# Delta-rule attention layer on one chip: gate stage and l2norms moved in the block head, two filters' spectral products separated

## The chip, the cores and the metric
One Trainium2 chip, 8 cores. Every core runs the same program on one of the 8 batch rows (2048 tokens of 1024 features); the cores exchange nothing. The metric is the device time in microseconds of the slowest core. The profile is of that core (core 5) in one execution.

## The reference
One layer with adaptive layer norm (shift, scale and gate from a conditioning row), an attention part and a feed-forward part. Shortened:

```
h = layernorm(x) * (1 + ca) + sa
q, k, v = [silu(causal_dwconv(h @ W, conv4))  for W in (Wq, Wk, Wv)]    # 4 heads x 256
beta = sigmoid(h @ Wb);  w_global = sigmoid(h @ Wg + bg);  p = softmax((h @ Wl + bl) / temp)
q, k = l2norm(q), l2norm(k)                        # per head
o_d  = delta rule over q, k, v, beta               # chunkwise, state S of 256 x 256 per head
local = p0 * v + p1 * fir_short(v) + p2 * fir_long(v)     # 3 and 31 taps, causal
o = rmsnorm(w_global * o_d + (1 - w_global) * local) @ Wo
x = x + ga * o
h = layernorm(x) * (1 + cb) + sb
x = x + gb * tanh(h @ W @ A1 @ A2 + bias)
```

## The kernel before
A core works through its 2048 tokens in 4 blocks of 512 (`for b in range(NB)`). A block has a head, four chunks of 128 tokens, and the feed-forward part.

**How the order is set.** Each stage is queued with `st(engine, counter, waits, instructions)`; every engine runs its stages in the order in which the program queues them, and a stage waits for the marks named in it. So an instruction that waits holds up everything queued behind it on its engine. A stage counts once, at its last instruction. Weight loads are issued from GpSimd's queue, each after the previous one has landed, two halves of `w_str` in turn.

**The head.** `ln_and_h` normalizes the block and leaves h in `h_blk`. `project` computes one of q, k, v: four groups of two column blocks (PSUM `ps_p`, `ps_q`), each group with two half loads of weights, 16 matmuls (L539), and two ScalarE copies into `z_blk` (L553), which also wait for the mark `z_free`. Then VectorE does the 4-tap convolution into `y_blk` (L565, L573), and ScalarE applies Silu (L585). `z_free` is set when the convolution has read `z_blk`. `l2norm` squares q or k (VectorE, L591), sums by matmul (L593), takes Ln and Exp on ScalarE (L600, L603), and for each of four heads copies the factor to all partitions by an fp32 matmul (L614), copies it to SBUF `rs_rep` (ScalarE, L620) and multiplies (VectorE, L624). `bgl_stage` computes the gates: 8 matmuls from `h_blk` (L637), a ScalarE copy of the logits into a part of `rs_rep` (L643), four transposes (L646), and a chain of small steps on VectorE and ScalarE (L652 to L692). The order is: project q, l2norm q, gates, project k, l2norm k, project v.

**A chunk.** K and v are transposed to token-major (L741, L757) and copied and scaled by beta (L748, L749, L764, L765). The two filters are applied as products in the frequency domain: forward transform (L775, L782), three copies (L790 to L792), then for the long (f = 0) and the short filter (f = 1) six VectorE products and sums each (L806 to L824), an inverse transform of the long one (L828), its ScalarE copy to `ls_tm` (L836), the same for the short one in the same PSUM (L838, L846), and the mix (L849, L855, L862). Then the output projection of the chunk before is queued (`emit_tail`: transposes, ScalarE copy L708, 16 matmuls L711, residual add L719). Then come the 128 x 128 triangular inverse by six squarings (L871 to L940), the delta rule with its state update (L950 to L1032), and the RMS norm of the result (L1043 to L1055). `z_blk` also serves as scratch (`wfm`, `attnT`) in the chunks.

Of the kernel before, what the change touches and what calls it, by code (L numbers as in the profile page):

```python
# [9 lines left out]
ALU = mybir.AluOpType  # L10
# [150 lines left out]
def build_nc():  # L161
# [40 lines left out]
    with _stack:  # L202
# [26 lines left out]
        kh_blk = _stack.enter_context(nc.sbuf_tensor("kh_blk", [128, 4096], BF16))  # L229
        v_blk = _stack.enter_context(nc.sbuf_tensor("v_blk", [128, 4096], BF16))  # L230
# [5 lines left out]
        zh_k = _stack.enter_context(nc.sbuf_tensor("zh_k", [128, 32], BF16))  # L236
        zh_v = _stack.enter_context(nc.sbuf_tensor("zh_v", [128, 32], BF16))
# [24 lines left out]
        xhat = _stack.enter_context(nc.sbuf_tensor("xhat", [128, 2048], BF16))  # L262
# [32 lines left out]
        PE = Ctr(_pe); DVE = Ctr(_dve); ACT = Ctr(_act)  # L295
        LD = Ctr(_ld, 16); GLD = Ctr(_gld, 16); ST = Ctr(_st, 16)
        LDX = Ctr(_ldx, 16); GLD1 = Ctr(_gld1, 16)
        st = sch.stage
# [44 lines left out]
        m_wh = wh_last  # L343
# [19 lines left out]
        for q in range(4):  # L363
# [44 lines left out]
        m_clamp = st("vector", DVE, [m_cl3], [  # L408
            lambda e: e.tensor_tensor(ga_row, absrow, sgnrow, ALU.mult)])
# [22 lines left out]
        m_gates = st("vector", DVE, [m_g3], [  # L432
            lambda e: e.tensor_tensor(gates_fm[:, 40:48], st6[:, 0:8], st6[:, 8:16], ALU.mult)])
# [22 lines left out]
        state = {  # L456
            "m_h": m_consts, "m_x": m_x,
            "wstr_free": m_consts,
            "psg_free": m_gates, "pstr_free": m_wofold,
            "pspq_free": [m_mod, m_mod],  # L460
            "psu_free": m_wh, "pso_free": m_gar, "ofm_free": m_hist0,
            "m_S": m_hist0, "m_vtmprev": m_hist0, "m_mix_done": m_hist0,
            "m_clamp": m_clamp,
            "ln_free": m_gates,
            "y_free": m_hist0,
            "z_free": m_hist0,
        }
# [121 lines left out]
        def l2norm(src, m_src):  # L589
            sq = st("vector", DVE, [m_src, state["y_free"]], [  # L590
                lambda e: e.tensor_tensor(y_blk[:], src[:], src[:], ALU.mult)])  # L591
            smm = st("tensor", PE, [sq, state["psg_free"]], [
                (lambda e, g=g: e.matmul(ps_g[0:4, 0:512], onesl2_sb[:, 4 * g:4 * g + 4],  # L593
                                         y_blk[:, 512 * g:512 * (g + 1)],
                                         start=(g == 0), stop=(g == 7)))
                for g in range(8)
            ])
            state["y_free"] = smm
            rt0 = st("scalar", ACT, [smm], [
                lambda e: e.activation(rs4[0:4, 0:512], ps_g[0:4, 0:512],  # L600
                                       AF.Ln, bias=epsc_sb[0:4, 1:2])])
            rt = st("scalar", ACT, [rt0], [
                lambda e: e.activation(rs4[0:4, 0:512], rs4[0:4, 0:512],  # L603
                                       AF.Exp, scale=epsc_sb[0:4, 4:5])])
            state["psg_free"] = rt
            rc = rt
            marks = []
            for h in range(4):
                half = h % 2
                waits = [rc, state["pso_free"]]  # L610
                if len(marks) >= 2:
                    waits.append(marks[-2])
                rep = st("tensor", PE, waits, [
                    (lambda e, h=h, half=half: e.matmul(  # L614
                        ps_o[:, 512 * half:512 * (half + 1)],
                        onehot4_sb[:, 128 * h:128 * (h + 1)], rs4[0:4, 0:512],
                        start=True, stop=True))
                ])
                evr = st("scalar", ACT, [rep], [
                    (lambda e, half=half: e.copy(rs_rep[:, 512 * half:512 * (half + 1)],  # L620
                                                 ps_o[:, 512 * half:512 * (half + 1)]))
                ])
                ap = st("vector", DVE, [evr], [
                    (lambda e, h=h, half=half: e.tensor_tensor(  # L624
                        src[:, 1024 * h:1024 * (h + 1)].rearrange("p (c t) -> p c t", c=2),
                        src[:, 1024 * h:1024 * (h + 1)].rearrange("p (c t) -> p c t", c=2),
                        rs_rep[:, 512 * half:512 * (half + 1)].unsqueeze(1)
                        .broadcast_to([128, 2, 512]),
                        ALU.mult))
                ])  # L630
                marks.append(ap)
            state["pso_free"] = marks[-1]
            return marks[-1]
# [93 lines left out]
        for b in range(NB):  # L727
            ln_and_h(b, 0)
            m_q = project(b, "wq", qh_blk, zh_q, 0)
            m_ql2 = l2norm(qh_blk, m_q)  # L730
            m_bgl = bgl_stage(m_ql2)
            m_k = project(b, "wk", kh_blk, zh_k, 32)
            m_kl2 = l2norm(kh_blk, m_k)
            m_v = project(b, "wv", v_blk, zh_v, 64)

            for n in range(NCB):
                cofs = 128 * n
# [49 lines left out]
                    for ns in range(2) for kc in range(2)  # L787
                ])
                exh = st("vector", DVE, [ffw], [
                    lambda e: e.tensor_copy(xhat[:, 0:1024], ps_u[:, 0:1024]),  # L790
                    lambda e: e.tensor_copy(xhat[:, 1024:1536], ps_g[:, 0:512]),
                    lambda e: e.tensor_copy(xhat[:, 1536:2048], ps_p[:, 0:512]),  # L792
                ])
# [7 lines left out]
                _yh = (yhat[:], yhat2)  # L801
                _whf = (whl_sb, whs_sb)
                _sc = (mscr[:, 0:1024], mscr[:, 1024:2048])
                cm1 = st("vector", DVE, [exh, m_wh, state["m_mix_done"], state["m_clamp"],
                                         state["psu_free"]],
                    [(lambda e, f=f: e.tensor_tensor(  # L806
                        _yh[f][:, 0:1024], xhat[:, 0:1024], _whf[f][:, 0:1024], ALU.mult))
                     for f in range(2)]
                  + [(lambda e, f=f: e.tensor_tensor(
                        _sc[f], xhat[:, 1024:2048], _whf[f][:, 1024:2048], ALU.mult))  # L810
                     for f in range(2)]
                  + [(lambda e, f=f: e.tensor_tensor(
                        _yh[f][:, 1024:2048], xhat[:, 0:1024], _whf[f][:, 1024:2048], ALU.mult))
                     for f in range(2)])
                cm2 = st("vector", DVE, [cm1],
                    [(lambda e, f=f: e.tensor_sub(
                        _yh[f][:, 0:1024], _yh[f][:, 0:1024], _sc[f]))
                     for f in range(2)])
                cm3 = st("vector", DVE, [cm2],
                    [(lambda e, f=f: e.tensor_tensor(  # L820
                        _sc[f], xhat[:, 1024:2048], _whf[f][:, 2048:3072], ALU.mult))
                     for f in range(2)])
                cm = st("vector", DVE, [cm3],
                    [(lambda e, f=f: e.tensor_add(  # L824
                        _yh[f][:, 1024:2048], _yh[f][:, 1024:2048], _sc[f]))
                     for f in range(2)])
                im = st("tensor", PE, [cm, state["psu_free"]], [
                    (lambda e, ns=ns, part=part: e.matmul(  # L828
                        ps_u[:, 512 * ns:512 * (ns + 1)],
                        (dftir_sb if part == 0 else dftii_sb)[:, :],  # L830
# [352 lines left out]
```

How the kernel before makes its waits and increments, by code:

```python
        def fn(e):  # L144
            for c, v in wlist:
                if v > 0:
                    e.wait_ge(c.h, v)
            last = None
            for g in emits:
                last = g(e)
                if per_instr:
                    last.then_inc(ctr.h, ctr.step)
            if not per_instr:
                last.then_inc(ctr.h, ctr.step)
# [985 lines left out]
        def fin(e):  # L1140
            e.wait_ge(ST.h, ST.n)
```

## Time and profile before

| what | value |
|---|---|
| median of 3 runs (lowest, highest) | 2979.19 us (2978.45, 2985.77) |
| the profiled execution | 2974.76 us, span on core 5 2973.2 us |
| spans of the 8 cores | 2966.5 to 2973.2 us |
| TensorE busy | 1234.3 us, 42% of the span |
| VectorE busy | 1040.0 us, 35% |
| ScalarE busy | 405.8 us, 14% |
| GpSimd busy | 120.6 us, 4% |
| granted TensorE clock, mean | 0.66 of full speed |

Engines are called PE (TensorE matmul), PEld (weight load), DVE (VectorE), ACT (ScalarE), POOL (GpSimd), SP in the rows. L539 is line 539 of the kernel. Times in the rows are microseconds from the span's start. The chain of waits is followed back from the last instruction, at each step to what released it.

### The profile page before, as it was taken

The numbers are of one execution on the slowest core, as the hardware profiler recorded it, in microseconds if no ns is written. First come the engines' busy times: TensorE is split into PE (matmuls) and PEld (weight loads), VectorE is DVE, ScalarE is ACT, GpSimd is POOL, SyncE is SP. The second block draws the span as 40 slices with busy tenths as digits, with TensorE's granted clock in tenths as the row PEclk, the third lists the DMA queues.
The fourth block names the chain that finished last, engine by engine and source line by source line (L and its number), as shares of the span: only waits on it lengthen the run. The fifth ranks groups of instructions, "written<-read, shape, count | busy, mean of one in ns | idle before, by whom it ended". The sixth has DMA issues, their size and how long they took to land.

```text
span 2973.2 us, 16737 instructions; the slowest of 8 cores (2966.5 to 2973.2 us)
## 1 busy us (share of the span) xinstructions
PE 1234.3 (42%) x5208; PEld 549.7 (18%) x5208; DVE 1040.0 (35%) x1904; ACT 405.8 (14%) x547; POOL 120.6 (4%) x232
## 2 busy tenths in 40 slices
PE   1223442444454442444354433344454344344444
PEld 0001111222212111222211111222211111222211
DVE  1002336555301334555301333555501233555501
ACT  0002211000112211000112121000022221000021
POOL 0010000000010000000010000000000000000000
PEclk9999665555576666565576666565577676555567
DMA  7442120000032111000033222000023222000023
GB/s 177 74 75 29 23 29 12 0 1 0 5 56 60 25 28 25 0 1 0 1 50 64 29 28 29 0 1 0 0 43 71 28 29 29 0 1 1 0 35 71
DMA packets 38650, 83.95 MB, mean 28 GB/s; under 512 B 5084, under 2 KB 5503, under 8 KB 38438
## 3 DMA queue, kind: packets, MB, share of 16 engines
q0 software_dynamic: 32624, 65.14, 15.2%
q1 hardware_dynamic: 5942, 17.74, 1.7%
q8 instruction: 47, 0.77, 0.1%
q14 instruction: 37, 0.30, 0.0%
HBM read 139.60 MB, written 8.39 MB: 50 GB/s over the span
## 4 chain that ended last, share of the span: by engine, by line
DVE 29%; PE 26%; DMA 26%; issue 9%; ACT 8%; DVEq 0%; ACTq 0%; POOLq 0%; POOL 0%
DMA w_str<-wf_a 8%; DVE y_blk L573 7%; DMA z_blk<-wmod 5%; DMA w_str<-wk 3%; DMA w_str<-wq 3%; DMA w_str<-wv 3%; DMA w_str<-wf_w 3%; PE ps_o L711 3%; DVE Pp L923 2%; PE ps_o L614 2%; PE ps_g L932 2%; DVE Qp L926 2%; ACT h_blk L508 2%; DVE st L474 1%; ACT y_blk L492 1%
## 5 line engine op out<-in xcount | busy, mean ns | idle before, releaser
L573 DVE SCALAR_TENSOR_TENSOR y_blk<-z_blk,convw_sb,y_blk 128x512 bf16<-128x512 bf16 x288 | 194.0, 746 | 4.5 <-DVE y_blk L573 0.5
L539 PE MATMUL ps_p<-h_blk,w_str 128*128 128x512 bf16 x384 | 127.6, 465 | 151.9 <-DMA w_str<-wk 49.3
L1111 DVE TENSOR_SCALAR y_blk<-y_blk,gates_fm 128x512 bf16<-128x512 bf16 x32 | 11.3, 353 | 493.7 <-ACT y_blk L1107 493.7
L539 PE MATMUL ps_q<-h_blk,w_str 128*128 128x512 bf16 x384 | 133.8, 485 | 0.0
L593 PE MATMUL ps_g<-y_blk,onesl_sb 128*4 128x512 bf16 x64 | 28.3, 621 | 225.0 <-DVE y_blk L591 225.0
L932 PE MATMUL ps_g<-Rt,Pp 128*128 128x128 bf16 x384 | 56.2, 300 | 141.6 <-DVE Qp L926 123.7
L502 PE MATMUL ps_tr<-eye_sb,y_blk 128*128 128x128 bf16 x256 | 32.4, 307 | 155.3 <-ACT y_blk L492 114.8
L940 DVE TENSOR_TENSOR Rt<-Rt,ps_g 128x512 bf16<-128x512 bf16 x96 | 66.0, 687 | 80.9 <-PE ps_g L932 80.9
L711 PE MATMUL ps_o<-wo_sb,ofm_sb 128*128 128x512 bf16 x256 | 84.9, 505 | 22.4 <-ACT ofm_sb L708 22.4
L757 PE MATMUL ps_tr<-eye_sb,v_blk 128*128 128x128 bf16 x128 | 16.2, 306 | 184.3 <-ACT v_blk L585 100.4
L828 PE MATMUL ps_u<-yhat,dftir_sb 128*128 128x512 bf16 x32 | 19.5, 609 | 176.1 <-DVE mix_b L824 176.1
L539 PEld LDWEIGHTS ps_p<-h_blk,w_str 128*128 128x128 bf16 x384 | 36.1, 108 | 241.0 <-issue 225.6
L978 ACT CAST dtiles<-ps_u 128x512 bf16<-128x512 f32 x16 | 9.4, 585 | 513.2 <-PE ps_u L970 513.2
L1079 POOL DMA_DIRECT2D w_str<-wf_w x32 | 16.9, 528 | 1519.5 <-PE ps_q L1088 1407.5
L923 DVE CAST Pp<-ps_p 128x512 bf16<-128x512 f32 x96 | 66.3, 690 | 27.0 <-PE ps_q L915 27.0
L553 ACT CAST z_blk<-ps_p 128x512 bf16<-128x512 f32 x48 | 28.1, 585 | 325.2 <-PE ps_q L539 325.2
L1088 PE MATMUL ps_p<-kh_blk,w_str 128*128 128x512 bf16 x128 | 43.5, 474 | 67.4 <-DMA w_str<-wf_a 52.4
L379 PE MATMUL ps_g<-z_blk,cfm_sb 128*1 128x512 bf16 x32 | 18.7, 584 | 125.6 <-DMA z_blk<-wmod 125.6
L562 DVE TENSOR_TENSOR z_blk<-zh_q 128x32 bf16<-128x32 bf16 x4 | 0.7, 176 | 200.5 <-ACT z_blk L553 200.5
L1088 PE MATMUL ps_p<-qh_blk,w_str 128*128 128x512 bf16 x128 | 44.5, 483 | 62.4 <-DMA w_str<-wf_a 58.3
L614 PE MATMUL ps_o<-rs,onehot_sb 4*128 4x512 f32 x64 | 58.1, 1069 | 24.9 <-ACT rs L603 24.9
L1088 PE MATMUL ps_p<-h_blk,w_str 128*128 128x512 bf16 x128 | 46.7, 503 | 52.2 <-DMA w_str<-wf_w 43.3
(224 smaller groups left out, 2447.5 us busy)
## 6 DMA issues: line engine op xcount, KB each, us to landing
w_str<-wf_a POOLq DMA_DIRECT2D x64, 256.0 KB, 3.8
z_blk<-wmod POOLq DMA_DIRECT2D x32, 384.0 KB, 4.4
x_tm<-x SPq DMA_DIRECT2D x1, 8192.0 KB, 31.1
w_str<-wq POOLq DMA_DIRECT2D x32, 256.0 KB, 3.8
w_str<-wk POOLq DMA_DIRECT2D x32, 256.0 KB, 3.8
w_str<-wv POOLq DMA_DIRECT2D x32, 256.0 KB, 3.8
w_str<-wf_w POOLq DMA_DIRECT2D x32, 256.0 KB, 3.8
out<-x_tm SPq DMA_DIRECT2D x4, 2048.0 KB, 6.6
```

The costliest lines, as they stand in the source:

```text
L474: (lambda e, n=n, hf=hf: e.bn_stats(st6[:, 12 * n + 6 * hf: 12 * n + 6 * hf + 6], x_tm[:, xofs + 1024 * n + 512 * hf: xofs + 1024 * n + 51 ...
L502: (lambda e, g=g, n=n: e.transpose(ps_tr[:, 512 * (g % 2) + 128 * n: 512 * (g % 2) + 128 * (n + 1)], y_blk[:, 1024 * n + 128 * g: 1024 * n ...
L508: (lambda e, g=g: e.activation(h_blk[:, 512 * g:512 * (g + 1)], ps_tr[:, 512 * (g % 2):512 * (g % 2) + 512], AF.Identity, bias=gates_fm[:, ...
L539: (lambda e, g=g, mh=mh, hb=hb, pp=pp: e.matmul(pp[:, 0:512], halves[hb][:, 256 * (g - 4 * hb) + 128 * mh: 256 * (g - 4 * hb) + 128 * mh + ...
L573: (lambda e, g=g, j=j: e.scalar_tensor_tensor(y_blk[:, 512 * g:512 * (g + 1)], z_blk[:, 516 * g + j + 1: 516 * g + j + 513], convw_sb[:, c ...
L614: (lambda e, h=h, half=half: e.matmul(ps_o[:, 512 * half:512 * (half + 1)], onehot4_sb[:, 128 * h:128 * (h + 1)], rs4[0:4, 0:512], start=T ...
L711: (lambda e, g=g, sl=sl: e.matmul(ps_o[:, 512 * sl:512 * (sl + 1)], ofm_sb[:, 128 * g:128 * (g + 1)], wo_sb[:, 1024 * g + 512 * sl: 1024 * ...
L923: (lambda e, pn=pnx: e.tensor_copy(Pp[:, 512 * pn:512 * (pn + 1)], ps_p[:, 0:512])),
L926: (lambda e, qn=qnx: e.tensor_copy(Qp[:, 512 * qn:512 * (qn + 1)], ps_q[:, 0:512])),
L932: (lambda e, h=h, pn=pnx, rc=rcur: e.matmul(ps_g[:, 128 * h:128 * (h + 1)], Pp[:, 512 * pn + 128 * h: 512 * pn + 128 * (h + 1)], Rt[:, 512 ...
L940: (lambda e, rc=rcur, rn=rnx: e.tensor_add(Rt[:, 512 * rn:512 * (rn + 1)], Rt[:, 512 * rc:512 * (rc + 1)], ps_g[:, 0:512]))
L1088: (lambda e, g=g, mh=mh, hb=hb, pp=pp, src=src: e.matmul(pp[:, 0:512], halves[hb][:, 256 * (g - 4 * hb) + 128 * mh: 256 * (g - 4 * hb) + 1 ...
```

## The change
Two parts. In the head, the gate stage is queued right behind the q projection, the k and v projections follow, and both l2norms stand behind them, q's first. The gate stage's copy of the logits, which writes `rs_rep`, no longer waits for l2norm of q but for a new mark, the last block's l2norm of k. In the chunk, the six products of the long filter are queued first and those of the short one behind them, with waits between the dependent steps of each (four stages per filter, in place of four for both together), and the long filter's inverse transform waits for its own six alone.

```
+            "rsrep_free": m_gates,
...
             m_q = project(b, "wq", qh_blk, zh_q, 0)
+            m_bgl = bgl_stage(state["rsrep_free"])
+            m_k = project(b, "wk", kh_blk, zh_k, 32)
+            m_v = project(b, "wv", v_blk, zh_v, 64)
             m_ql2 = l2norm(qh_blk, m_q)
-            m_bgl = bgl_stage(m_ql2)
-            m_k = project(b, "wk", kh_blk, zh_k, 32)
             m_kl2 = l2norm(kh_blk, m_k)
-            m_v = project(b, "wv", v_blk, zh_v, 64)
+            state["rsrep_free"] = m_kl2
...
-                cm1 = st("vector", DVE, [exh, m_wh, state["m_mix_done"], state["m_clamp"],
-                                         state["psu_free"]],
-                    [(lambda e, f=f: e.tensor_tensor(
-                        _yh[f][:, 0:1024], xhat[:, 0:1024], _whf[f][:, 0:1024], ALU.mult))
-                     for f in range(2)]
...
-                cm2 = st("vector", DVE, [cm1],
...
-                cm3 = st("vector", DVE, [cm2],
...
-                cm = st("vector", DVE, [cm3],
...
-                im = st("tensor", PE, [cm, state["psu_free"]], [
+                cmw = [exh, m_wh, state["m_mix_done"], state["m_clamp"],
+                       state["psu_free"]]
+                cmf = [None, None]
+                for f in range(2):
+                    c1 = st("vector", DVE, (cmw if f == 0 else [cmf[0]]), [
+                        (lambda e, f=f: e.tensor_tensor(
+                            _yh[f][:, 0:1024], xhat[:, 0:1024], _whf[f][:, 0:1024], ALU.mult)),
+                        (lambda e, f=f: e.tensor_tensor(
+                            _sc[f], xhat[:, 1024:2048], _whf[f][:, 1024:2048], ALU.mult)),
+                        (lambda e, f=f: e.tensor_tensor(
+                            _yh[f][:, 1024:2048], xhat[:, 0:1024], _whf[f][:, 1024:2048], ALU.mult)),
+                    ])
+                    c2 = st("vector", DVE, [c1], [
+                        (lambda e, f=f: e.tensor_sub(
+                            _yh[f][:, 0:1024], _yh[f][:, 0:1024], _sc[f]))])
+                    c3 = st("vector", DVE, [c2], [
+                        (lambda e, f=f: e.tensor_tensor(
+                            _sc[f], xhat[:, 1024:2048], _whf[f][:, 2048:3072], ALU.mult))])
+                    cmf[f] = st("vector", DVE, [c3], [
+                        (lambda e, f=f: e.tensor_add(
+                            _yh[f][:, 1024:2048], _yh[f][:, 1024:2048], _sc[f]))])
+                cm = cmf[1]
+                im = st("tensor", PE, [cmf[0], state["psu_free"]], [
```

## Rows read from the trace of the kernel before

**Rows 1.** Page, chain that ended last, share of the span by engine

```profile
DVE 29%; PE 26%; DMA 26%; issue 9%; ACT 8%; DVEq 0%; ACTq 0%; POOLq 0%; POOL 0%
```

**Rows 2.** Chain of waits, second block, q to k: start, duration, what

```profile
1005.49 3.62 ACT qh_blk L585
...
1029.41 0.58 ACT rs_rep L643
...
1030.38 1.84 PE ps_p L539 x4
```

**Rows 3.** Chain of waits, second block, k to v and the first chunk

```profile
1084.88 3.62 ACT kh_blk L585
...
1094.80 1.28 ACT L600
...
1105.24 1.82 PE ps_p L539 x4
...
1109.36 3.57 DMA w_str<-wv
...
1130.70 3.94 DMA w_str<-wv
...
1138.23 0.19 DVE z_blk L562
...
1157.26 1.28 ACT L585
...
1162.42 1.02 PE ps_tr L757 x8
```

**Rows 4.** Timeline, head of the second block and a chunk's begin: start, duration, instruction, idle before

```profile
624.60 0.68 DVE L748 COPY dtiles<-ps_tr 128x1024 bf16<-128x1024 bf16 x1
...
626.56 1.01 PE L757 MATMUL ps_tr<-eye_sb,v_blk 128*128 128x128 bf16 x8 [6.46 <-DVE dtiles L749]
...
984.30 0.53 POOL L529 DMA_DIRECT2D w_str<-wk  x1 [5.93 <-PE ps_q L539]
...
988.69 0.53 POOL L529 DMA_DIRECT2D w_str<-wk  x1 [3.86 <-DMA w_str<-wk]
...
1026.52 0.69 DVE L624 TENSOR_TENSOR qh_blk<-qh_blk,rs_rep 128x1024 bf16<-128x1024 bf16 x1 [1.01 <-ACT rs_rep L620]
...
1036.09 0.58 ACT L553 CAST z_blk<-ps_p 128x512 bf16<-128x512 f32 x1
```

**Rows 5.** Timeline, filter part of the first block's third chunk

```profile
636.29 0.69 DVE L806 TENSOR_TENSOR yhat<-xhat,whl_sb 128x1024 bf16<-128x1024 bf16 x1
636.89 0.68 DVE L806 TENSOR_TENSOR mix_b<-xhat,whs_sb 128x1024 bf16<-128x1024 bf16 x1
...
639.30 0.68 DVE L812 TENSOR_TENSOR mix_b<-xhat,whs_sb 128x1024 bf16<-128x1024 bf16 x1
640.09 0.69 DVE L816 TENSOR_TENSOR yhat<-yhat,mix_s 128x1024 bf16<-128x1024 bf16 x1
...
643.49 0.68 DVE L824 TENSOR_TENSOR mix_b<-mix_b,mix_s 128x1024 bf16<-128x1024 bf16 x1
...
644.32 0.59 PE L828 MATMUL ps_u<-yhat,dftir_sb 128*128 128x512 bf16 x1 [11.00 <-DVE mix_b L824]
...
645.13 0.63 PE L828 MATMUL ps_u<-yhat,dftir_sb 128*128 128x512 bf16 x1
...
646.34 1.01 ACT L836 CAST ls_tm<-ps_u 128x1024 bf16<-128x1024 f32 x1 [23.44 <-PE ps_u L828]
647.49 0.58 PE L838 MATMUL ps_u<-mix_b,dftir_sb 128*128 128x512 bf16 x1 [1.30 <-ACT ls_tm L836]
```

**Rows 6.** Chain of waits, end of the first block's first chunk

```profile
546.36 1.28 ACT L1050
```

**Rows 7.** Chain of waits, output projection inside a block and at its end

```profile
651.62 5.53 PE ps_o L711 x16
...
777.84 5.57 PE ps_o L711 x16
```

More of the change, by code:

```diff
@@ L803, in build_nc @@
                 _sc = (mscr[:, 0:1024], mscr[:, 1024:2048])
-                cm1 = st("vector", DVE, [exh, m_wh, state["m_mix_done"], state["m_clamp"],
-                                         state["psu_free"]],
-                    [(lambda e, f=f: e.tensor_tensor(
-                        _yh[f][:, 0:1024], xhat[:, 0:1024], _whf[f][:, 0:1024], ALU.mult))
-                     for f in range(2)]
[L809 to L814, printed above, removed]
@@ L815, in build_nc @@
-                cm2 = st("vector", DVE, [cm1],
-                    [(lambda e, f=f: e.tensor_sub(
-                        _yh[f][:, 0:1024], _yh[f][:, 0:1024], _sc[f]))
-                     for f in range(2)])
-                cm3 = st("vector", DVE, [cm2],
-                    [(lambda e, f=f: e.tensor_tensor(
-                        _sc[f], xhat[:, 1024:2048], _whf[f][:, 2048:3072], ALU.mult))
-                     for f in range(2)])
-                cm = st("vector", DVE, [cm3],
-                    [(lambda e, f=f: e.tensor_add(
-                        _yh[f][:, 1024:2048], _yh[f][:, 1024:2048], _sc[f]))
-                     for f in range(2)])
```

## The prediction
> **What bounds the kernel now.** I read the page's chain of waits first, because the busy shares name no full engine: no engine is near a full span, and the chain that ends last is shared between VectorE, TensorE and DMA [rows 1]. So the kernel is a long hand-over from engine to engine, and an edit is worth what it takes out of that chain, not what it takes off an engine. I then read the chain in order of time through the head of the second block (rows of the block b = 1): from the q projection to the k projection [rows 2], from k to v and on to the first chunk [rows 3]. The reader should see that each projection is a strict sequence: weights and matmuls, eviction, 19 us of convolution on VectorE, Silu, and for q and k an l2norm before TensorE starts the next projection. The timeline gives the ends of single steps there [rows 4], and then the filter part of one chunk [rows 5]: twelve VectorE products in a row, then inverse transform, copy, inverse transform, copy, while VectorE waits. The change touches both stretches: the head (4 times) and the filter part (16 times). I take the second block's head and the first block's third chunk for all of their kind.
>
> **The head, q to k (4 times).** Silu of q ends at 1005.49 + 3.62 = 1009.11; the copy of the gate logits starts at 1029.41 and k's first matmul at 1030.38 [rows 2]. The 20.3 us between are l2norm of q (to the last multiply's end, 1026.52 + 0.69 = 1027.21, so 18.1 us [rows 4]) and the gate matmuls. After the change the gate matmuls stand right behind q's last projection matmul and run under the convolution. But k does not start under the convolution: TensorE's next instructions are the gate transposes, they wait for the copy of the logits on ScalarE, and that copy is queued behind Silu of q, which waits for the convolution. So k's matmuls start 0.97 us (1030.38 - 1029.41) behind the end of Silu: 20.3 us earlier. The rest of the gate chain goes on under k's first group as now; k's first eviction already stands behind that chain on ScalarE (1036.09 [rows 4], 5.7 us behind k's first matmul) and keeps that distance. **-20.3.**
>
> **The head, k to v.** Silu of k ends at 1088.50; v's first matmul comes at 1105.24, and v's convolution begins at 1138.23, 33.0 us on [rows 3]. After the change v's matmuls stand directly behind k's on TensorE. Their first group (two half loads) is loaded and multiplied under k's convolution, and the second group's two halves are loaded there too. Its eviction has to wait: z_blk is free only after k's convolution, and ScalarE has Silu of k in front. So TensorE stops at v's second group until Silu of k and the first copy are done (1088.50 + about 0.75 = 1089.2). That is 16.0 us before 1105.24, and from there four loads are left in place of six. A load's period is (1130.70 - 1109.36) / 5 = 4.27 us [rows 3], so another 8.5 us are saved: **-24.6**. The two extra loads issued under VectorE's convolution have 17 us to land; the first k load is issued just ahead of q's convolution today, and the second follows 4.39 us later [rows 4], one normal period, so the convolution does not hold a load back.
>
> **The head, what is put behind v.** Silu of v then follows Silu of k with only copies between, so its table load (1157.26, 1.28 us [rows 3]) goes: **-1.28**. Both l2norms now follow it with nothing beside them: VectorE, TensorE and ScalarE pass one result around. The first costs what it costs now, 18.1; the second lacks its table load (1.28, at 1094.80 [rows 3]), 16.8. K's transposes and the two VectorE copies behind them, which now run under v's convolution and Silu, become exposed: 0.2 to start, 1.02 for eight transposes (as v's at 1162.42 [rows 3]), 0.1 to the copies, then 1.96 from the first copy to the next transposes (624.60 to 626.56 [rows 4]), about 3.3, against 0.26 now between Silu's end and v's transposes (1157.26 + 1.28 + 3.62 = 1162.16 to 1162.42). Sum: 18.1 + 16.8 + 3.3 - 0.3 = **+37.9**. In the first chunk the reciprocal root no longer needs its table load (1.28, at 546.36 [rows 6]), since Ln and Exp ran last; VectorE waits for it, so **-1.28**.
>
> One block: -20.3 - 24.6 - 1.28 + 37.9 - 1.28 = -9.5; four blocks: **-38 us**. So the move is mostly a transfer of 35 us of l2norm to another exposed place. The gain is the gate matmuls, v's hidden loads and three table loads.
>
> **The filter part (16 times).** The twelve products keep their count and sizes. Two that follow without a wait start 0.60 apart (636.29, 636.89); where a wait on the previous stage stands between, 0.79 (639.30, 640.09) [rows 5]. Before there are three such waits, after seven: the last product ends 4 x 0.19 = 0.76 us later, at 643.49 + 0.68 + 0.76 = 644.93. The first filter's last product is then the sixth: 636.29 + 2 x 0.60 + 3 x 0.79 = 639.86, done 0.69 later at 640.55. Its inverse transform and copy (now 644.32 to 646.34 + 1.01 = 647.35, 3.03 us [rows 5]) run from 640.70 to 643.73 under the second filter's products. The second inverse transform starts 0.15 behind the last product, at 645.08, in place of 647.49: **-2.41 us**. Everything behind it keeps its order: the copy of the short filter, the output projection's transposes and matmuls of the chunk before, the residual add; VectorE's mix waits for that copy and moves along. With 16 chunks: **-38.6 us**. The work that hides the first filter's transform and copy is the second filter's six products; they outlast it by 1.35 us (643.73 to 645.08), and what is lost of that cover beyond 1.35 comes off the gain.
>
> The added waits are the one place where a page speaks otherwise. The rows show 0.19 us for a stage boundary [rows 5]. The Trainium skill, "VectorE: DVE Perf Modes", section "The DRAIN you can't avoid", says that the pipeline is emptied after every operation anyway and that a semaphore between operations costs nothing extra. By that the split would cost 0 and the filter part would give 3.17 us a chunk, 51 us in all. The rows of this trace disagree with it, so the sum keeps 0.76; the other is a rival below.
>
> **Clock.** A filter part in which TensorE is used in shorter pieces could lose the granted clock. What shows against it is the output projection: after a busy TensorE it takes 5.53 us for 16 matmuls, and at the end of a block, where TensorE stood idle before the transposes, 5.57 [rows 7]. So its speed does not hang on what ran before. I take 0. The upper bound is that all 16 matmuls keep the spacing of the inverse transform's, which run at the lower level: (645.13 - 644.32) / 2 = 0.405 [rows 5], 6.5 us for 16, so +1.0 per chunk; below 0 I see nothing, since those matmuls already speed up in mid-group.
>
> **Sum.** Profiled execution 2974.8 us (span 2973.2 and 1.6 around it) - 38.0 - 38.6 = 2898.2. The profiled execution is 4.4 us under the median of the runs, 2979.2; the same difference taken from that median gives 2902.6. I forecast **2900 us**, between the two.
>
> **Rivals.**
> *The added waits are free* (above): VectorE's boundary costs nothing when the data dependence would have stalled it anyway; against it, 0.60 and 0.79 in the same stage. 2900 - 16 x 0.76 = 2888.
> *The clock is lost in the output projection*, at its bound: 2900 + 16 x 1.0 = 2916.
> *The head gives nothing*: a hidden wait of about 9.5 us per block, for instance v's second group held by a late half load. For it: loads come one after another, 4.27 each. Against it: they have the whole convolution. 2938.
> *The filter part gives nothing*: the first inverse transform is not done when the second is ready, a loss of the 1.35 us cover and 2.4 us more. 2939.
> *K starts under q's convolution*, if the logits' copy ran ahead of Silu: two loads more are hidden per block, 4 x 8.5 = 34. ScalarE's order speaks against it. 2866.
> *Slower*: k and v do not come forward, and the l2norm pair is pure addition. The place is the queue of ScalarE and TensorE between Silu and the next projection: if TensorE's transposes or v's first eviction waited for something that ends only where the l2norm ended before, 44.9 us per block would stay. 2900 + 4 x 44.9 = 3080. It decides from 19 us per block not regained (76.6 / 4). No row shows such a releaser.
> *Neither half does anything*: the two losses just named together, 2977.
>
> **How the numbers follow.** Forecast 62 in 100; free waits 10; clock 10; head nothing 6; filter nothing 3; k under the convolution 3; slower 4; no change 2. Faster by over 0.3% (9 us, about what a measurement of this kernel can tell from no change) is all but the last two: 94; same 2; slower 4. The range takes the forecast, the free waits and the lost clock, 82 in 100, with some 4 us at the ends for the two bases of the sum: 2884 to 2925.
>
> **What would show it.** In the profile after: k's first matmul about 1 us behind the end of Silu of q, not under the convolution; TensorE stopped between v's first and second group until a z_blk copy behind Silu of k; no table load between Silu of k and Silu of v; 35 us of l2norm behind Silu of v; in a chunk, ls_tm's copy finished before the last of twelve products, and the second inverse transform 0.15 us behind that product, 8.8 us after the first product's start (11.2 now). The table loads fall by three per block, or by four if Silu and Sigmoid share a table (that one lies in the gate chain, under k's first group). The prediction is wrong if v's convolution starts much later than 25 us behind Silu of k, or if the two l2norms together take clearly more or less than 35 us.

## The result, and the profile after

The changed kernel takes 2897.6 us (median of 8 runs, 2893.8 to 2902.9), the kernel before 2981.9 on the same chip: ratio 0.9713, 95% interval 0.9699 to 0.9727, so 81 to 90 us less. 2900 were forecast; the working gave 76.6 us of gain, so 5 to 13 us are a surplus over it. From 2981.9 the working would have given 2905; the forecast came nearer because it started from the profiled execution and the first three runs, some 5 us lower, and that part is luck. A second comparison on another chip gives 0.9726 (0.9710 to 0.9742). The chips differ by more than half a per cent (the kernel before takes 2982 us on one, 2963 to 2965 on others), so every comparison below is a ratio within one chip, and microseconds are worked out from it.

The page's chain of the changed kernel, by engine, is almost what it was [rows 1], on a shorter span:

```profile
span 2896.6 us, 16793 instructions; the slowest of 8 cores (2877.1 to 2896.6 us)
...
DVE 30%; PE 26%; DMA 26%; issue 10%; ACT 8%; DVEq 0%; ACTq 0%; POOLq 0%; POOL 0%
```

The head of the second block, chain of waits of the changed kernel (start, duration, what), against [rows 2, 3]:

```profile
987.40 3.62 ACT qh_blk L586
991.01 0.47 ACT rs_rep L644
...
991.88 1.84 PE ps_p L540 x4
...
1045.83 3.62 ACT kh_blk L586
1049.44 0.48 ACT z_blk L554
1050.06 1.87 PE ps_p L540 x4
...
1054.24 3.71 DMA w_str<-wv
...
1066.96 3.89 DMA w_str<-wv
...
1094.08 3.63 ACT v_blk L586
1097.80 2.30 DVE y_blk L592
...
1103.99 1.28 ACT L601
...
1115.83 2.29 DVE y_blk L592
...
1131.97 0.70 DVE kh_blk L625
1132.81 1.03 PE ps_tr L743 x8
...
1135.96 1.03 PE ps_tr L759 x8
```

K's first matmul comes 0.86 us behind Silu of q (991.02 to 991.88; 21.3 before) and not under the convolution. V's second group starts right behind the copy that follows Silu of k, with four loads left, and v's convolution begins at 1075.04, 25.6 us behind Silu of k (49.7 before). Between Silu of k and Silu of v there is no table load: 48.25 us from one to the other, 73.67 before. Behind Silu of v the two l2norms pass from engine to engine alone, 1097.71 to 1132.67, 35.0 us; v's transposes start 38.25 us behind that Silu, 0.26 before.

The filter part of one chunk, timeline, against [rows 5]:

```profile
622.87 0.68 DVE L811 TENSOR_TENSOR yhat<-xhat,whl_sb 128x1024 bf16<-128x1024 bf16 x1
...
626.45 0.69 DVE L825 TENSOR_TENSOR yhat<-yhat,mix_s 128x1024 bf16<-128x1024 bf16 x1
...
627.29 0.58 PE L829 MATMUL ps_u<-yhat,dftir_sb 128*128 128x512 bf16 x1 [7.39 <-DVE yhat L825]
...
629.58 1.01 ACT L837 CAST ls_tm<-ps_u 128x1024 bf16<-128x1024 f32 x1 [20.10 <-PE ps_u L829]
...
630.84 0.69 DVE L825 TENSOR_TENSOR mix_b<-mix_b,mix_s 128x1024 bf16<-128x1024 bf16 x1
...
631.78 0.58 PE L839 MATMUL ps_u<-mix_b,dftir_sb 128*128 128x512 bf16 x1 [2.63 <-DVE mix_b L825]
```

The long filter's copy ends at 630.59, 0.94 us ahead of the last product's end (631.53); the second inverse transform starts 8.91 us behind the first product, 11.20 before, and what it waited for is VectorE (the bracket), no longer the copy.

### The profile page after: what moved, and what is told of

The parts are those of the page before. It is cut to its first block, busy times and chain, and to the rows that moved or that the text cites. A ratio compares the mean times of both kernels' runs of the same rounds, so it can differ in the third digit from the quotient of the medians.

```text
span 2896.6 us, 16793 instructions; the slowest of 8 cores (2877.1 to 2896.6 us)
## 1 busy us (share of the span) xinstructions
PE 1238.6 (43%) x5208; PEld 550.8 (19%) x5208; DVE 1045.5 (36%) x1904; ACT 389.8 (13%) x535; POOL 120.7 (4%) x232
## 4 chain that ended last, share of the span: by engine, by line
DVE 30%; PE 26%; DMA 26%; issue 10%; ACT 8%; DVEq 0%; ACTq 0%; POOLq 0%; POOL 0%
DMA w_str<-wf_a 8%; DVE y_blk L574 7%; DMA z_blk<-wmod 5%; DMA w_str<-wq 3%; DMA w_str<-wk 3%; DMA w_str<-wf_w 3%; PE ps_o L712 3%; DVE Pp L924 2%; DMA w_str<-wv 2%; PE ps_g L933 2%; PE ps_o L615 2%; DVE Qp L927 2%; ACT h_blk L509 2%; DVE st L475 1%; PE ps_p L540 1%
## 5 line engine op out<-in xcount | busy, mean ns | idle before, releaser
L540 PE MATMUL ps_p<-h_blk,w_str 128*128 128x512 bf16 x384 | 135.9, 490 | 212.7 <-ACT z_blk L554 59.4
L540 PE MATMUL ps_q<-h_blk,w_str 128*128 128x512 bf16 x384 | 139.6, 502 | 0.0
L933 PE MATMUL ps_g<-Rt,Pp 128*128 128x128 bf16 x384 | 56.2, 301 | 141.3 <-DVE Qp L927 123.3
L540 PEld LDWEIGHTS ps_p<-h_blk,w_str 128*128 128x128 bf16 x384 | 37.4, 112 | 303.2 <-issue 290.3
L1089 PE MATMUL ps_p<-h_blk,w_str 128*128 128x512 bf16 x128 | 47.1, 506 | 55.2 <-DMA w_str<-wf_w 44.7
L909 PE MATMUL ps_p<-Pp,Qp 128*128 128x128 bf16 x384 | 58.0, 302 | 16.5 <-DVE Rt L894 16.5
L933 PEld LDWEIGHTS ps_g<-Rt,Pp 128*128 128x128 bf16 x384 | 33.5, 127 | 163.1 <-issue 163.1
```

The source lines that it names most:

```text
L540: (lambda e, g=g, mh=mh, hb=hb, pp=pp: e.matmul(pp[:, 0:512], halves[hb][:, 256 * (g - 4 * hb) + 128 * mh: 256 * (g - 4 * hb) + 128 * mh + ...
L909: (lambda e, h=h, pc=pcur, qc=qcur: e.matmul(ps_p[:, 128 * h:128 * (h + 1)], Qp[:, 512 * qc + 128 * h: 512 * qc + 128 * (h + 1)], Pp[:, 51 ...
L933: (lambda e, h=h, pn=pnx, rc=rcur: e.matmul(ps_g[:, 128 * h:128 * (h + 1)], Pp[:, 512 * pn + 128 * h: 512 * pn + 128 * (h + 1)], Rt[:, 512 ...
L1089: (lambda e, g=g, mh=mh, hb=hb, pp=pp, src=src: e.matmul(pp[:, 0:512], halves[hb][:, 256 * (g - 4 * hb) + 128 * mh: 256 * (g - 4 * hb) + 1 ...
```

## The experiments

For the stages I took, in each core's trace, the times between the same instructions of every block, and give the mean of 8 cores as a sum over the 4 blocks: Silu of q to Silu of k, Silu of k to Silu of v, end of Silu of v to v's first transposes, and from there to the feed-forward part's norm (the four chunks). There is one trace of each kernel, and none of the kernel before on these two chips.

```
us, 4 blocks        q to k   k to v   v to transposes   chunks
head_only            232.4    192.2       150.6         1212.2     } one chip
fir_only             307.6    295.5         1.0         1171.2     }
fir_waits_only       309.1    295.9         1.0         1223.0     }
k_under_conv         193.0    190.8       149.3         1165.5     }
after_again          231.5    192.6       150.4         1161.7     } a second chip
l2_in_loads          199.1    199.5         1.0         1174.0     }
l2_preload           193.3    193.9         4.4         1164.1     }
```

**The head alone (head_only).** The kernel before, with this edit only:

```
+            "rsrep_free": m_gates,
...
             m_q = project(b, "wq", qh_blk, zh_q, 0)
-            m_ql2 = l2norm(qh_blk, m_q)
-            m_bgl = bgl_stage(m_ql2)
+            m_bgl = bgl_stage(state["rsrep_free"])
...
-            m_kl2 = l2norm(kh_blk, m_k)
             m_v = project(b, "wv", v_blk, zh_v, 64)
+            m_ql2 = l2norm(qh_blk, m_q)
+            m_kl2 = l2norm(kh_blk, m_k)
+            state["rsrep_free"] = m_kl2
```

> Only the head of the change (gates behind q, both l2norms behind v); the filter part as before. By the working of the prediction: -9.5 us per block, -38 us in all, ratio 0.987. Rival A (the surplus of some 8 us of the whole change over the forecast comes from the head): -45 to -47. Rival B (the head gives nothing): 0. In its profile the output projection (16 matmuls per chunk) should take what it takes before, 84.9 us busy in all.

Measured: 0.9892 (0.9874 to 0.9909), -32 us (-27 to -37). The surplus is not here; the head gives a little less than its sum. By stages, against fir_only, whose head is the old one: q to k -75.2, k to v -103.3, transposes +149.6; expected -81, -104 and +152. Of the output projection's busy sum, expected at 84.9, the cores show 83.7 to 90.2.

**The filter part alone (fir_only).** The second half of the diff above.

> Only the filter part of the change; the head as before. By the working: -2.41 us per chunk, -38.6 us in all, ratio 0.987. Rival A (surplus from the head): the same -38.6. Rival C (the surplus sits in the output projection, which runs at a higher granted clock when the first inverse transform has moved ahead): -43 to -47, with the output projection's busy sum near 80 us in place of 84.9.

Measured: 0.9851 (0.9834 to 0.9867), -44 us (-39 to -49). More than the sum said, as rival C has it. Against head_only, on the same chip, the chunks are 41.0 us shorter, and head_only has one table load per block less in them (5.1), so 46: 36.6 between a chunk's first product and its second inverse transform (2.29 per chunk), 4.9 between the delta rule's masked product and its mix (the stage of the delta rule's output, shown below), and 5.1 between the second inverse transform and the first product of the triangular inverse, where the output projection stands. So rival C's place is at most a part of it: the output projection's busy sum is 79.7 to 87.4 on the cores, mean 83.2, against 87.4 in the mean for head_only but 83.4 in the trace of before, from another chip (80.3 to 85.7). Alone the halves multiply to 0.9745 against 0.9713 and 0.9726 measured together; the intervals leave nothing sure for an interaction.

**The added waits alone (fir_waits_only).** As fir_only, but with no overlap:

```
-                im = st("tensor", PE, [cmf[0], state["psu_free"]], [
+                im = st("tensor", PE, [cm, state["psu_free"]], [
```

> The filter part with the new order and its seven waits on VectorE, but the long filter's inverse transform still waits for all twelve products: the added waits alone. By the working: four more boundaries of 0.19 us per chunk, +0.76 x 16 = +12 us, ratio 1.004. Rival (the page's rule that a semaphore between VectorE operations costs nothing extra): 0.

Measured: 1.0021 (1.0011 to 1.0031), +6 us (3 to 9): neither 12 nor 0. Timeline, first product and inverse transform of a chunk:

```profile
631.55 0.69 DVE L809 TENSOR_TENSOR yhat<-xhat,whl_sb 128x1024 bf16<-128x1024 bf16 x1
...
640.36 0.59 PE L827 MATMUL ps_u<-yhat,dftir_sb 128*128 128x512 bf16 x1 [11.78 <-DVE mix_b L823]
```

8.81 us from one to the other, 8.03 before [rows 5]: the four waits cost 0.78 us, as the sum had it. The Trainium skill ("VectorE: DVE Perf Modes", section "The DRAIN you can't avoid") measured on eight tensor copies that a semaphore after each costs nothing extra; that does not hold for these products. It is not only the data dependence: the second filter's first product reads nothing that the first filter wrote, and still starts 0.80 us behind the product that it waits for (635.13 to 635.93), where 0.60 is the step without a wait. Half of 0.78 x 16 = 12.5 is given back further on. Groups by line, slowest core of head_only and of fir_waits_only, the same 128 matmuls of the delta rule's output behind the squarings (busy us, mean ns):

```profile
L1005 PE MATMUL ps_o<-S_sb,qh_blk 128*128 128x256 bf16 x128 | 38.5, 403 | 16.9 <-DVE z_blk L994 16.9
```

```profile
L1002 PE MATMUL ps_o<-S_sb,qh_blk 128*128 128x256 bf16 x128 | 31.9, 352 | 16.9 <-DVE z_blk L991 16.9
```

Over the 8 cores these matmuls take 376 to 404 ns in head_only (mean 388) and 333 to 368 in fir_waits_only (mean 351), with nothing of theirs changed. The granted clock from the first to the last of a chunk's eight, a mixture of the two levels 1.2 and 2.4 GHz, is 0.55 of full speed in the one and 0.65 in the other. The stage of the delta rule's output falls from 58.4 to 52.7 us in 16 chunks, and these 5.7 us are about the half that came back.

Fir_only against fir_waits_only prices the overlap itself, chunks 1171.2 against 1223.0: -51.8 us, 3.24 a chunk, where 3.17 was worked out. Of it 3.04 lie between the first product and the second inverse transform, and 0.24 behind that in the stretch with the output projection (busy sum 87.6 against 83.2 in the mean of the cores), whose own instructions are the same.

**A delay without waits (extra1, extra2).** The kernel before, with one or two products more per chunk, which nobody reads (extra2; extra1 has `range(1)`):

```
+                  + [(lambda e, f=f: e.tensor_tensor(
+                        z_blk[:, 2048 + 1024 * f:3072 + 1024 * f], xhat[:, 0:1024], _whf[f][:, 0:1024], ALU.mult))
+                     for f in range(2)]
```

> The kernel before, with one product more per chunk on VectorE ahead of the inverse transforms (a copy of the first product, into a part of z_blk that the chunk does not use): a delay of 0.60 us per chunk without any other order or wait. Open is why the added waits, 0.8 us per chunk in VectorE's rows, cost only 6 us in all, with the delta rule's matmuls shorter behind them. If the delay itself shifts the later matmuls against the granted clock: clearly less than 0.60 x 16 = 9.7 us, near 4 to 5. If the give-back belongs to the new order of the products: the full 9.7.

> The same with two products more, 1.21 us per chunk. If the delay itself shifts the matmuls against the granted clock: less than 1.21 x 16 = 19.4 us by some 5 or more, or a give-back that does not grow evenly with the delay. If not: 19.4.

Measured: 1.0016 (1.0007 to 1.0025), +4.7 us (2.1 to 7.4), and 1.0042 (1.0029 to 1.0054), +12.4 us (8.6 to 16.0). Of 9.7 and 19.4 us of work on the chain, 5 and 7 come back (2 to 8, and 3 to 11). So a part of a delay can come back without a wait and without a new order. But the traces do not show that it comes back in the same place. In them the 128 matmuls of the delta rule take 380 and 371 ns in the mean of the cores (granted clock 0.57 and 0.59), against 385 (0.56) in the trace of before, from another chip, and the stage of the delta rule's output takes 57.1 and 56.2 us against 57.6: that is 1 us or less and 1 to 2 us of the 5 and 7. Where the rest comes back is not shown. Nor does a longer front explain the faster matmuls: fir_only's front, from the first product to the second inverse transform, is 2.3 us per chunk shorter than the old one, and its matmuls take 356 ns (0.63). All seven traces with the new order of the products have these matmuls at 342 to 364 ns, all four with the old order at 371 to 388; the runs do not separate that order from the timing that follows from it.

**K's first group under the convolution (k_under_conv).** The changed kernel, with the gate stage cut in two: matmuls, copy and transposes are queued ahead of Silu of q, the rest inside q's l2norm.

```
-            m_bgl = bgl_stage(state["rsrep_free"])
+            m_q = project(b, "wq", qh_blk, zh_q, 0, {"pre_sl": gates_a})
+            gt["evb"] = bgl_bias(gt["tmm"])
...
+            m_ql2 = l2norm(qh_blk, m_q, gates_b, gates_c)
```

> The whole change, and the gates' copy and transposes moved ahead of Silu of q on ScalarE and TensorE, so that nothing stands between q's and k's projection matmuls on TensorE but work that is ready; the rest of the gate chain runs between the steps of q's l2norm. If the gate transposes behind Silu are what keeps k's first group from the convolution: another 8.5 us per block as for v, -34 us against the changed kernel, about -119 against the kernel before, ratio 0.960. Rival (the head's loads or the gate chain set the pace in any case): as the changed kernel, ratio 0.971.

Measured: 0.9579 (0.9563 to 0.9594), -125 us against before. Against head_only on that chip, the stage from q to k falls from 232.4 to 193.0, 9.9 us per block (8.5 expected), and nothing else in the head moves by 2 us. Chain of waits, second block:

```profile
962.34 3.62 ACT qh_blk L592
965.96 0.48 ACT z_blk L558
966.57 1.87 PE ps_p L543 x4
...
970.75 3.70 DMA w_str<-wk
...
983.22 3.70 DMA w_str<-wk
```

What follows Silu of q is now k's first eviction, k's second group, and four loads, as for v. So the gates' copy queued behind Silu on ScalarE, with the transposes that wait for it on TensorE, was what kept k out of the convolution.

**The l2norms inside the loads (l2_in_loads).** The stages of each l2norm are queued between the matmul groups of the projection that follows it: the square at its start, the sums behind the second group, Ln and Exp behind that group's eviction, two scalings behind the third group and two behind the fourth:

```
+                return {"start": lambda: l2.square(m_src), ("ev", 0): ev0,
+                        ("mm", 1): l2.sums, ("ev", 1): ev1, ("mm", 2): mm2,
+                        ("ev", 2): ev2, ("mm", 3): mm3, ("ev", 3): ev3, "pre_sl": post}
...
-            m_ql2 = l2norm(qh_blk, m_q)
-            m_kl2 = l2norm(kh_blk, m_k)
+            m_k = project(b, "wk", kh_blk, zh_k, 32, window(lq, m_q, True))
+            m_v = project(b, "wv", v_blk, zh_v, 64, window(lk, m_k, False))
```

> As k_under_conv, and each l2norm is spread over the next projection: square and sums while the second group's matmuls run, Ln and Exp and the four scalings between the load-bound matmul groups of k (for q) and of v (for k). The theory says that the 35 us of l2norm behind Silu of v are exposed only because nothing is queued beside them, and that the projections' load waits have room for them (2.3 us in each load period of 4.3). Expected per block: -37 for the pair and the transposes behind it, +1 to +2 for matmuls that l2norm's matmuls delay, twice, +2.6 for two table loads that come back; -32 x 4 = about -130 to -140 against k_under_conv, about 0.912 against the kernel before. Rival (the l2norm matmuls and copies in the loads' gaps hold the weight loads up by as much as they hide, 17 us per projection): as k_under_conv, 0.958.

Measured: 0.9175 (0.9161 to 0.9188), -244 us against before and about 163 less than the changed kernel on that chip (0.9726); the gain over k_under_conv (0.9579) is 120 us by the ratios, the expectation's 0.912 was a little too good. The 150 us behind Silu of v are gone, and the two stages with a projection grow by 1.5 and 2.2 us per block against k_under_conv (193.0 to 199.1, 190.8 to 199.5, traces of two chips), of which a table load that comes back ahead of Silu is 1.28. Timeline, k's projection in the second block:

```profile
944.43 1.02 PE L543 MATMUL ps_p<-h_blk,w_str 128*128 128x512 bf16 x4 [0.89 <-DMA w_str<-wk]
944.72 0.53 POOL L533 DMA_DIRECT2D w_str<-wk  x1 [3.59 <-DMA w_str<-wk]
...
949.05 0.53 POOL L533 DMA_DIRECT2D w_str<-wk  x1 [3.80 <-DMA w_str<-wk]
...
951.00 3.78 PE L632 MATMUL ps_o<-rs,onehot_sb 4*128 4x512 f32 x4
...
953.13 0.53 POOL L533 DMA_DIRECT2D w_str<-wk  x1 [3.55 <-PE ps_o L632]
```

The scalings' matmuls (L632) stand between two groups, and the next load is still issued 4.08 us behind the last one: the loads are not held up.

**Tables loaded ahead (l2_preload).** One element of Silu ahead of each Silu, and of Ln behind the last:

```
+            st("scalar", ACT, [], [
+                lambda e: e.activation(itrow_sb[0:1, 0:1], epsc_sb[0:1, 5:6], AF.Silu)])
...
+            st("scalar", ACT, [], [
+                lambda e: e.activation(itrow_sb[0:1, 1:2], epsc_sb[0:1, 3:4], AF.Ln, scale=epsc_sb[0:1, 3:4])])
```

> As l2_in_loads, with a Silu of one element queued on ScalarE ahead of each convolution's end and a Ln of one element behind Silu of v, so that the activation tables are loaded while ScalarE is idle. If an exposed table load costs the 1.28 us that its row shows: four per block, -20 us against l2_in_loads. If each switch costs 2.66 us, as the Trainium skill states on ScalarE: Activation LUTs (What ACT_TABLE_LOAD costs), -42 us. Rival (the loads are hidden already): 0.

Measured: 0.9099 (0.9085 to 0.9112), -267 us against before; against l2_in_loads -22 us by the two ratios, about 20 expected. Groups by line, table loads at Silu, of l2_in_loads and of l2_preload (busy, mean ns, idle before):

```profile
L592 ACT ACT_TABLE_LOAD x12 | 15.4, 1283 | 212.4 <-DVE y_blk L579 194.2 <-DVE zh_v L587 18.2
```

```profile
L592 ACT ACT_TABLE_LOAD x12 | 15.4, 1283 | 0.2
```

The loads are as many and as long, but no longer behind the convolution. What came back is 1.4 us for each of 16 loads, near the row's 1.28 and not the 2.66 that the Trainium skill gives for a switch ("ScalarE: Activation LUTs", section "What ACT_TABLE_LOAD costs"). The two stages with one such load per block agree, 1.45 and 1.40 us less. The load at Silu of v pays less: v's transposes then wait for the copies of k, and 0.85 us per block are lost again there (1.0 to 4.4 in the table).

**The changed kernel again (after_again).**

> The changed kernel once more, on the chip of the next two, so that sums can be compared on one chip. If the two halves add (0.9892 and 0.9851 alone), 0.9745 against the kernel before; if they help each other, the 0.9713 of the first comparison.

Measured: 0.9726 (0.9710 to 0.9742), between the two.

## Why the prediction was right, step by step

The time and both mechanisms held; two terms of the sum were mis-sized, in opposite directions, so that the sum came out closer than its terms, which is luck.

- *K earlier by 20.3 us.* The shift is as said: mean over all blocks and cores, k's first matmul stands 20.97 us behind Silu of q before and 0.86 after. But the term took k's projection as unchanged behind it, and that grew: from k's first matmul to Silu of k 52.3 to 53.0 us in the traces with the old head, 53.4 to 53.8 in those with the new. Before, l2norm's and the gates' matmuls ran just ahead of k's first 16 matmuls, which took 3.2 to 8.9 us from the first start to the last, 4.6 to 5.0 in the mean of each trace; after, TensorE stood idle, and they take at least 4.6, 5.4 in the mean. That is about half of the growth; the rest is not located. The step gave 18.8 us per block (75.2 / 4), 1.5 less than its term. The sampled block began that group at the lower level, 1.2 GHz (granted clock 0.50, 1.84 us for the first four matmuls [rows 2]), as the blocks do after the change, and hid most of the difference: its 16 matmuls took 5.2 us.
- *V's group and loads hidden, one table load gone: -25.9.* Measured -25.8 (103.3 / 4).
- *The l2norm pair behind v: +37.9.* Measured +37.4 (149.6 / 4).
- *The table load in the first chunk: -1.28.* From the delta rule's mix to the RMS-scaled output of a block's first chunk: 9.90 us in fir_only, 8.60 in head_only; -1.3.
- *The filter part: -2.41 per chunk, its waits at 0.76.* The waits cost 0.78 in VectorE's rows, and the overlap gave 3.24 in the chunks (3.17 forecast). From the first product to the second inverse transform the step gave 2.29 per chunk. But the added waits cost the kernel only 6 us in place of 12, and the trace has 5.7 of the difference in the delta rule's output, whose matmuls ran at a higher clock. This is the step "Clock, I take 0", with "below 0 I see nothing": the delta rule's matmuls were not looked at. The output projection was weighed, and "its speed does not hang on what ran before", read from two rows, does not hold either: with its own instructions unchanged its granted clock is 0.65 in fir_waits_only and 0.69 in fir_only, its busy sum 87.6 and 83.2.
- *Sum.* Head: -75.2 - 103.3 + 149.6 - 5.1 = -34 by the stages and -32 by the runs, forecast -38; filter part alone -44, forecast -38.6. The two errors partly cancel.
- *Rivals.* Free waits: excluded by the row, half true in the time, for another reason. K under the convolution: excluded for this order, and true as soon as the copy is moved ahead of Silu. The slower case: no sign of it.

Open: why the delta rule's matmuls get the higher clock more often behind the new order of the products. A longer front is not the condition, since fir_only shows it with a shorter one, and the two delays give back time without much of it.

## What to carry to other kernels

Moving an exposed chain to another exposed place is worth only what it lets start earlier; price both places, and look for a stage that waits for loads and has room for the chain. That was worth 30 us per block here (120 / 4), the reordering of the head itself 8. And an engine's own order decides: one copy queued behind one activation kept the next projection's first group of matmuls from starting under the convolution (9.9 us per block). A sample of one block carries its own clock; a term that rests on matmuls should be a mean over the blocks.

## What the runs showed of the hardware that was not expected

Extra work ahead of the inverse transforms is partly free in this kernel: 0.60 and 1.21 us of extra VectorE work per chunk cost 4.7 us (2.1 to 7.4) and 12.4 us (8.6 to 16.0) in 16 chunks where the work sums to 9.7 and 19.4. The same 128 matmuls of the delta rule take 388 ns in the mean of the cores in head_only (granted clock 0.55) and 351 in fir_waits_only (0.65), where only instructions of other stages differ. A wait between two of these VectorE products costs 0.19 to 0.20 us even where the second needs nothing from the first. And a one-element activation ahead of time takes a 1.28 us table load off the path (1.4 us for each of 16).
